# Keys and values staged in DRAM with a row's four tiles one behind the other

## The chip, the cores and the metric

The kernel runs on one core of a Trainium2 chip. The metric is the device time of one execution in microseconds; lower is better. The kernel before was run three times: median 568.12 us, from 563.62 to 568.17 us.

## The reference, cut to what matters

The input x is 32 sequences of 256 tokens of 128 features, float32. Four layers follow one another, each with a layer norm in front and a residual behind: windowed softmax attention (16 query heads, 2 key/value heads of 8 features), a feed-forward layer whose inner matrices are butterflies, linear attention, and the same feed-forward layer again. The change touches the first one alone:

```
q = (x @ Wq + bq) -> 16 heads of 8;  k = (x @ Wk + bk), v = (x @ Wv + bv) -> 2 heads of 8
k, v are padded by 16 zero tokens on both sides of the sequence
block of 32 queries n attends the 64 padded keys 32n .. 32n+63, masked to u in [t, t+32)
out = softmax(q k^T over those) v ;  x = x + out @ Wo + bo
```

Each group of 8 query heads shares one key head, and neighbouring windows overlap by half.

## The kernel before, in words

The 8192 tokens are cut into 16 groups of 512 (four tiles of 128 tokens, two sequences). The program is a software pipeline written out by hand: every engine has a function `turn(t)`, and in turn t it does a step of group t - lag, in an order fixed in the code. Turns 0 to 5 or so fill the pipeline (and TensorE composes the butterfly matrices, products named X, beside it); after them each turn has the same work of about ten groups' stages, and the last turns drain it. Engines wait for each other by counting semaphores (`Count`).

Keys and values of a group take this way. TensorE forms them for the four tiles, one below the other, in one PSUM bank (`attention_kv`, line 616): tile j stands in partitions 32j to 32j+31, of which the first 16 are key features, the other 16 value features, and each row holds 160 tokens (128 and the 16 on either side). VectorE adds the bias and clears the padding into `kv_t` [128, 160] (`attention_kv_out`, line 1020). SyncE stores `kv_t` to a DRAM tensor `kv_rows`, in two alternating copies (`store_keys`, line 326). When the store has landed, SyncE reads it back twice: `spread_keys` (line 335) with eight transfers, one for each query head h of a key head, that put the 16 key rows in partitions h, h+8, ... of `kx`, four tiles side by side, so each row of 640 numbers comes in four pieces of 160 numbers (640 B); and `spread_values` (line 347), one turn later, with eight transfers of 8 rows with four pieces of 64 numbers (256 B). `scores` on TensorE (line 531, products W.S0 to W.S3) reads `kx`; its first one of a group, W.S0, waits for all eight key transfers.

SyncE issues every transfer of the steady pipeline itself, in this order in each turn: the probabilities of tiles 2 and 3 copied between neighbouring partitions (`spread_probs`, line 355, four transfers of 32 partitions with 2 KB each a tile), values, store of keys and values, store of the result (`store_y`, line 362), probabilities of tile 0, keys, probabilities of tile 1, load of x (line 309). Each waits first for its own condition and so holds back all that stand behind it: `spread_probs(g, 0)` for ScalarE's exponentials (line 852), `spread_keys` for the landing of the store and for the last scores product of the group before (W.S3), the load of x for GpSimd (line 429). GpSimd masks the copied probabilities (`probs_parted`, line 459), which TensorE then multiplies with the values (line 548). VectorE works on the scores in line 1070 and after.

In turn 2 `spread_keys` also sends two loads of constants (`load_constants`); the first transfer of values waits for one of them. The first column of the table of rows below tells the time from the start of the profiled span.

Of the kernel before, what the change touches and what calls it, by code (L numbers as in the profile page):

```python
# [8 lines left out]
F32 = mybir.dt.float32  # L9
# [6 lines left out]
HEADS, KV, HD = 16, 2, 8  # L16
HPK = HEADS // KV
# [3 lines left out]
P = 128  # L21
TSPAN = P + 2 * PAD
TILES = 4
# [93 lines left out]
def due(t, lag, first=0, last=NG - 1):  # L117

    return (t - lag,) if first <= t - lag <= last else ()
# [24 lines left out]
def window_and_linear_attention_with_butterfly_ffn(  # L144
    nc, x, first_c, later_c, outer_c, vones_c, w_exp_t, w_con, up_m, down_m, out,
):
    with ExitStack() as ctx:
        def sb(name, shape, dt=F32):
            return ctx.enter_context(nc.sbuf_tensor(name, shape, dt))

        def sem(name):
            return ctx.enter_context(nc.semaphore(name))
# [49 lines left out]
        kv_t = sb("kv_t", [P, TSPAN])  # L202
        kx = sb("kx", [P, HPK, TILES * TSPAN])
# [58 lines left out]
        pool_step = Count(sem("pool_step"), POOL_STEPS)  # L262
        normed = Count(sem("normed"), NORMED)
        biased = Count(sem("biased"), BIASED)
        kv_rows = nc.dram_tensor("kv_rows", [2, P, TSPAN], F32).ap()
        kv_out = Count(sem("kv_out"), [("P.ko", 0)], 16)
        x_in = [sem(f"x_in{i}") for i in range(2)]
        kx_in = Count(sem("kx_in"), [("P.kx", 0)], 16 * HPK)
        spread = [Count(sem(f"spread{j}"), [(f"W.d{j}", 0)], 16 * 4) for j in range(TILES)]
# [6 lines left out]
        def x_of(g, s):  # L276
            return x_p[g % 2] if s == "P" else xs[s]
# [3 lines left out]

        def keys_of(g):

            return kv_rows[g % 2].rearrange("(j r) n -> r j n", j=TILES)[0:KV * HD]

        def values_of(g, kv):
            return kv_rows[g % 2].rearrange("(j r) n -> r j n", j=TILES)[KV * HD + kv * HD:KV * HD + (kv + 1) * HD]

        def outer_stage(eng, src, dst, tmp, coef, stage, step, seen):

# [11 lines left out]
        @block.sync  # L302
        def _(sp):
            def load_x(g):

                sp.wait_ge(normed.sem, normed.after(g - 2, "P.xn"))
                sp.wait_ge(biased.sem, biased.after(g - 2, "P.xb"))
                if g != 1:
                    sp.dma_start(x_of(g, "P")[:], x_v[g]).then_inc(x_in[g % 2], 16)
                if g == 0:  # L310
                    sp.dma_start(first[:], first_c).then_inc(first_in, 16)
                    sp.dma_start(x_of(1, "P")[:], x_v[1]).then_inc(x_in[1], 16)

            def load_constants():

                sp.dma_start(vx_t[:], vones_c.rearrange("p (a n) -> p a n", a=1).to_broadcast([P, TILES, P])
                             ).then_inc(vones_in, 16)
                sp.dma_start(later[:], later_c).then_inc(later_in, 16)

            def store_keys(g):  # L320

                own = drained[BANK["P.kv"]]
                sp.wait_ge(own.sem, own.after(g, "P.kv"))
                sp.wait_ge(kx_in.sem, kx_in.after(g - 2, "P.kx"))
                sp.wait_ge(v_in.sem, v_in.after(g - 2, "P.v"))
                sp.dma_start(kv_rows[g % 2], kv_t[:]).then_inc(kv_out.sem, 16)

            def spread_keys(g):

                sp.wait_ge(kv_out.sem, kv_out.after(g, "P.ko"))  # L330
                sp.wait_ge(kx_cleared, 2)

                sp.wait_ge(product.sem, product.after(g - 1, *SCORES))
                for h in range(HPK):
                    sp.dma_start(kx[h:P:HPK, h].rearrange("d (j n) -> d j n", j=TILES), keys_of(g)
                                 ).then_inc(kx_in.sem, 16)
                if g == 0:
                    load_constants()

            def spread_values(g):  # L340
                sp.wait_ge(kv_out.sem, kv_out.after(g, "P.ko"))
                sp.wait_ge(vones_in, 16)
                sp.wait_ge(vec.sem, vec.after(g - 1, "W.vx"))
                for i in range(4):
                    for kv in range(KV):
                        c = WINDOW[kv][i & ~1] + i % PARTS
                        sp.dma_start(vx_t[32 * i:32 * i + HD, :, kv * SPAN:(kv + 1) * SPAN],
                                     values_of(g, kv)[:, :, 32 * c:32 * c + SPAN]).then_inc(v_in.sem, 16)

            def spread_probs(g, j):  # L350

                sp.wait_ge(probs.sem, probs.after(g, f"W.E{j}"))
                for i in range(4):
                    own, other = slice(32 * i, 32 * i + 32), slice(32 * (i ^ 1), 32 * (i ^ 1) + 32)
                    sp.dma_start(probs_t[other, j, i % PAIR].rearrange("p k h t -> p (k h t)"),
                                 probs_t[own, j, i % PAIR].rearrange("p k h t -> p (k h t)")
                                 ).then_inc(spread[j].sem, 16)

            def store_y(g):
                own = drained[BANK["G.down"]]  # L360
                sp.wait_ge(own.sem, own.after(g, "G.down"))
                sp.dma_start(y_v[g], xs["G"][:]).then_inc(y_out.sem, 16)

            def turn(t):
                for g in due(t, 4):
                    spread_probs(g, 2)
                    spread_probs(g, 3)
                for g in due(t, 3):
                    spread_values(g)
                for g in due(t, 2):  # L370
                    store_keys(g)
                for g in due(t, 8):
                    store_y(g)
                for g in due(t, 3):
                    spread_probs(g, 0)
                for g in due(t, 2):
                    spread_keys(g)
                for g in due(t, 3):
                    spread_probs(g, 1)
                for g in due(t, 0):  # L380
                    load_x(g)

            for t in range(TURNS):
                turn(t)
            sp.wait_ge(y_out.sem, 16 * NG)
# [965 lines left out]
```

## Time and profile before

| | |
|---|---|
| median of 3 runs | 568.12 us (563.62 to 568.17) |
| profiled execution | 568.07 us, of which the span is 566.3 us |
| TensorE (PE) busy | 521.8 us, 92% of the span |
| GpSimd (POOL) | 451.9 us, 80% |
| VectorE (DVE) | 436.6 us, 77% |
| ScalarE (ACT) | 352.2 us, 62% |
| 16 DMA engines | mean 69 GB/s; SyncE's queue took 23.9% of their time |
| granted TensorE clock | 0.988 on average |

Engines are named as the profile does: PE for TensorE's products, PEld for its weight loads, SPq for SyncE's sequencer, which issues the transfers. A row of an issue tells how long the sequencer was at it, not when the data landed. "x8" in a row of the timeline means that eight such instructions stood in it one behind the other. A bracket at its end tells how long the engine had been idle before and what ended that.

### The profile page before, as it was taken

The page shows a single profiled execution, that of the slowest core. Times are in us where ns is not written, and L with a number is a line of the kernel's source. Part 1 is how long each engine was busy: PE and PEld are TensorE (multiplying, and loading weights), DVE is VectorE, ACT ScalarE, POOL GpSimd, SP SyncE. Part 2 cuts the span into 40 slices and gives each one's busy share as a digit, 9 for nine tenths or more (in the row PEclk, how much of TensorE's full clock was granted, in tenths as well). Part 3 has the DMA queues.
Part 4 walks back from the last instruction along what each step waited for, and adds up shares of the span by engine and source line. Part 5 has one row for each costly group of instructions (what it writes and reads, how often), then busy time and mean ns, then how long its engine had stood idle before and what let it go on. Part 6 is the DMA issues. An engine that isn't in the chain of part 4 may idle for free.

```text
span 566.3 us, 14624 instructions
## 1 busy us (share of the span) xinstructions
PE 521.8 (92%) x5048; PEld 344.3 (61%) x5048; DVE 436.6 (77%) x1256; ACT 352.2 (62%) x570; POOL 451.9 (80%) x651
## 2 busy tenths in 40 slices
PE   3866888979999999999999999999999999999876
PEld 2623344546666676766667667566676767677654
DVE  7277979998898989889898888888988888664330
ACT  1323464755876767676776685876767676836632
POOL 6343788989898998999999989898998787877531
PEclk9969999998999999999999999999999999999999
DMA  8414233231222232222223232222222222100001
GB/s 312 139 46 99 62 79 89 59 80 44 68 69 65 58 77 69 68 69 70 71 71 77 68 79 68 63 68 65 57 71 58 69 56 66 39 20 20 2 20 37
DMA packets 50186, 39.14 MB, mean 69 GB/s; under 512 B 12480, under 2 KB 39616, under 8 KB 50112
## 3 DMA queue, kind: packets, MB, share of 16 engines
q1 hardware_dynamic: 47664, 33.99, 23.9%
q10 hardware_dynamic: 2448, 4.22, 2.1%
q8 instruction: 40, 0.66, 0.5%
q14 instruction: 34, 0.28, 0.2%
HBM read 15.89 MB, written 5.51 MB: 38 GB/s over the span
## 4 chain that ended last, share of the span: by engine, by line
PE 79%; DVE 8%; POOL 5%; issue 3%; ACT 2%; ACTq 2%; SPq 1%; DMA 0%; DVEq 0%; POOLq 0%
PE ring L563 20%; PE ring L575 18%; PE ps_s L531 9%; PE ring L512 6%; PE ring L586 5%; PE ps_o L548 4%; PE ring L606 4%; PE ring L646 3%; PE ring L623 2%; POOL probs_t L459 2%; PE ring L595 2%; PE ring L666 1%; DVE merged L1083 1%; PE ring L616 1%; DVE ps_s L1070 1%
## 5 line engine op out<-in xcount | busy, mean ns | idle before, releaser
L459 POOL TENSOR_TENSOR probs_t<-probs_t,first 128x1024 f32<-128x1024 f32 x64 | 151.5, 2368 | 10.8 <-DMA probs_t<-probs_t 10.8
L852 ACT ACTIVATE probs_t<-merged_t 128x1024 f32<-128x1024 f32 x64 | 67.1, 1048 | 54.2 <-DVE merged_t L1090 46.2
L833 ACT ACT_TABLE_LOAD x58 | 74.4, 1283 | 10.9 <-issue 9.8
L531 PE MATMUL ps_s<-kx,q_t 64*32 64x512 f32 x1024 | 71.5, 615 | 8.0 <-DVE merged L1083 5.3
L563 PE MATMUL ring<-xT_G,w1b 128*128 128x512 f32 x128 | 66.3, 608 | 1.7 <-ACT xT_G L821 1.6
L575 PEld LDWEIGHTS ring<-w,hid_G 128*128 128x128 f32 x512 | 59.5, 192 | 10.0 <-issue 6.7
L575 PE MATMUL ring<-w,hid_G 128*128 128x128 f32 x512 | 60.0, 275 | 1.7 <-ACT hid_G L843 1.7
L563 PE MATMUL ring<-xT_F,w1b 128*128 128x512 f32 x128 | 59.9, 611 | 0.4 <-ACT xT_F L821 0.4
L575 PE MATMUL ring<-w,hid_F 128*128 128x128 f32 x512 | 60.0, 275 | 0.0
L575 PEld LDWEIGHTS ring<-w,hid_F 128*128 128x128 f32 x512 | 58.6, 192 | 0.5 <-issue 0.4
L843 ACT ACTIVATE hid_G<-ring,b 128x512 f32<-128x512 f32 x64 | 43.5, 681 | 17.1 <-PE ring L563 17.1
L1070 DVE COPY_PREDICATED ps_s<-first,ps_s 128x512 f32<-128x512 uint32 x64 | 43.7, 684 | 7.9 <-PE ps_s L531 7.9
L843 ACT ACTIVATE hid_F<-ring,b 128x512 f32<-128x512 f32 x64 | 43.4, 682 | 9.3 <-PE ring L563 7.8
L1097 DVE STREAM_TRANSPOSE ps_o<-ps_o 128x512 f32<-128x512 f32 x64 | 45.7, 714 | 0.2 <-PE ps_o L548 0.2
L548 PE MATMUL ps_o<-probs_t,vx 64*32 64x256 f32 x1024 | 42.3, 387 | 3.7 <-POOL probs_t L459 2.0
L1077 DVE TENSOR_REDUCE rowmax<-ps_s 128x16 f32<-128x512 f32 x64 | 43.1, 673 | 2.4 <-issue 0.2
L1083 DVE TENSOR_TENSOR merged<-ps_s,rowmax 128x512 f32<-128x512 f32 x64 | 43.8, 685 | 1.3
L1090 DVE STREAM_TRANSPOSE merged_t<-merged 128x512 f32<-128x512 f32 x64 | 44.5, 695 | 0.4
L563 PEld LDWEIGHTS ring<-xT_F,w1b 128*128 128x128 f32 x128 | 23.3, 192 | 30.3 <-issue 29.4
L563 PEld LDWEIGHTS ring<-xT_G,w1b 128*128 128x128 f32 x128 | 20.7, 190 | 22.5 <-ACT xT_G L821 12.4
L548 PEld LDWEIGHTS ps_o<-probs_t,vx 64*32 64x32 f32 x1024 | 15.2, 106 | 30.0 <-issue 21.8
L606 PEld LDWEIGHTS ring<-later,xT_L 128*128 128x128 f32 x128 | 22.9, 189 | 15.4 <-issue 11.3
(116 smaller groups left out, 1080.6 us busy)
## 6 DMA issues: line engine op xcount, KB each, us to landing
probs_t<-probs_t SPq DMA_DIRECT2D x256, 64.0 KB, 2.0
kx<-kv_rows SPq DMA_DIRECT2D x128, 40.0 KB, 2.2
x_P<-in_x SPq DMA_DIRECT2D x16, 256.0 KB, 3.3
out_x<-x_G SPq DMA_DIRECT2D x16, 256.0 KB, 2.4
vx_t<-kv_rows SPq DMA_DIRECT2D x128, 8.0 KB
up_s<-in_up_m ACTq DMA_DIRECT2D x7, 256.0 KB, 7.7
down_s<-in_down_m ACTq DMA_DIRECT2D x7, 256.0 KB, 7.7
kv_rows<-kv_t SPq DMA_DIRECT2D x16, 80.0 KB, 1.7
```

The costliest lines, as they stand in the source:

```text
L459: nc.gpsimd.tensor_tensor(parts, parts, keep.rearrange("p (a t) -> p a t", a=1).to_broadcast([P, PAIR * HEADS, WIN]), ALU.mult).then_inc(p ...
L531: last = nc.tensor.matmul(ps_s[32 * i:32 * i + 32, a], q_t[half, P * j + 32 * c:P * j + 32 * c + 32], kx[half, :, TSPAN * j + 32 * c:TSPAN ...
L548: last = nc.tensor.matmul(ps_o[32 * c:32 * c + 32, a, 0:HPK * WIN], vx[rows, j, a, s], probs_t[rows, j, s, a], start=True, stop=True)
L563: nc.tensor.matmul(bank(name)[:], w1b[:, P * c:P * (c + 1)], x_t[s][:], start=True, stop=True).then_inc(product.sem, 1)
L575: last = nc.tensor.matmul(bank(name)[:, P * j:P * (j + 1)], hid[s][:, c, P * j:P * (j + 1)], w2[:, c], start=(c == 0), stop=(c == CH - 1))
L606: last = nc.tensor.matmul(bank(name)[:, 2 * P * i:2 * P * (i + 1)], x_t["L"][:, P * j:P * (j + 1)], wl_s[:, P:3 * P], start=True, stop=True)
L833: nc.scalar.activation(unused[:, i:i + 1], half[0:1, 0:1], function)
L843: nc.scalar.activation(hid[s][:, c], bank(name)[:], ACT.Gelu, bias=b1[:, c:c + 1]).then_inc(drained[BANK[name]].sem, 1)
L852: nc.scalar.activation(probs_t[:, j].rearrange("p s k h t -> p s (k h t)"), scores.to_broadcast([P, PAIR, HEADS * WIN]), ACT.Exp).then_inc ...
L1070: nc.vector.copy_predicated(merged_s, last_half.bitcast(mybir.dt.uint32).rearrange("p (a t) -> p a t", a=1) .to_broadcast([P, HEADS, WIN]) ...
L1083: nc.vector.tensor_tensor(merged[:, j % 2].rearrange("p k h t -> p (k h) t"), halves()[0], m, ALU.subtract).then_inc(drained["S"].sem, 1)
L1097: nc.vector.transpose(ps_o[:, :, 0:HPK * WIN], ps_o[:, :, 0:HPK * WIN]).then_inc(vec.sem, 1)
```

## The change

The DRAM tensor gets 32 rows of 640 numbers in place of 128 rows of 160, so that the four tiles of a feature stand one behind the other in its row. The store becomes four transfers, one a tile (32 partitions of 640 B each, to rows that are 2560 B apart), and the semaphore that tells of it counts 64 instead of 16 a group. A key transfer reads 16 rows of 2560 B whole. A value transfer reads the same pieces as before from other places. SyncE's order and everything on the other engines stay.

```diff
-        kv_rows = nc.dram_tensor("kv_rows", [2, P, TSPAN], F32).ap()
-        kv_out = Count(sem("kv_out"), [("P.ko", 0)], 16)
+        kv_rows = nc.dram_tensor("kv_rows", [2, 2 * KV * HD, TILES * TSPAN], F32).ap()
+        kv_out = Count(sem("kv_out"), [("P.ko", 0)], 16 * TILES)
...
         def keys_of(g):
 
-            return kv_rows[g % 2].rearrange("(j r) n -> r j n", j=TILES)[0:KV * HD]
+            return kv_rows[g % 2][0:KV * HD]
 
         def values_of(g, kv):
-            return kv_rows[g % 2].rearrange("(j r) n -> r j n", j=TILES)[KV * HD + kv * HD:KV * HD + (kv + 1) * HD]
+            return kv_rows[g % 2][KV * HD + kv * HD:KV * HD + (kv + 1) * HD].rearrange("r (j n) -> r j n", j=TILES)
...
                 sp.wait_ge(v_in.sem, v_in.after(g - 2, "P.v"))
-                sp.dma_start(kv_rows[g % 2], kv_t[:]).then_inc(kv_out.sem, 16)
+                for j in range(TILES):
+                    sp.dma_start(kv_rows[g % 2][:, TSPAN * j:TSPAN * (j + 1)], kv_t[32 * j:32 * j + 32]
+                                 ).then_inc(kv_out.sem, 16)
...
                 for h in range(HPK):
-                    sp.dma_start(kx[h:P:HPK, h].rearrange("d (j n) -> d j n", j=TILES), keys_of(g)
+                    sp.dma_start(kx[h:P:HPK, h], keys_of(g)
                                  ).then_inc(kx_in.sem, 16)
```

## Rows read from the trace of the kernel before

**Rows 1.** The page, part 1: busy time, share of the span, instructions.

```profile
PE 521.8 (92%) x5048; PEld 344.3 (61%) x5048; DVE 436.6 (77%) x1256; ACT 352.2 (62%) x570; POOL 451.9 (80%) x651
```

**Rows 2.** Stretches: us, then each engine's busy time, TensorE's clock, DMA share, GB/s.

```profile
20.00:40.00 20.00, 15.21 (x118) 9.76 (x126) 9.10 (x21) 5.95 (x11) 6.35 (x14) 0.83 0.35 94
...
255.00:285.00 30.00, 30.00 (x309) 20.18 (x308) 25.99 (x77) 21.61 (x36) 27.59 (x41) 1.00 0.28 70
```

**Rows 3.** The page, part 6: transfers, KB each, median us from issue to landing.

```profile
probs_t<-probs_t SPq DMA_DIRECT2D x256, 64.0 KB, 2.0
kx<-kv_rows SPq DMA_DIRECT2D x128, 40.0 KB, 2.2
...
kv_rows<-kv_t SPq DMA_DIRECT2D x16, 80.0 KB, 1.7
```

**Rows 4.** Issues by source line: sequencer's time ns min/median/max, first and last start.

```profile
L335 SPq DMA_DIRECT2D kx<-kv_rows x128: 542/595/1899, 18.7 to 451.7; - x128
...
L347 SPq DMA_DIRECT2D vx_t<-kv_rows x128: 264/301/1347, 27.0 to 469.4; - x128
...
L326 SPq DMA_DIRECT2D kv_rows<-kv_t x16: 337/349/1008, 17.1 to 440.2; - x16
...
L355 SPq DMA_DIRECT2D probs_t<-probs_t x256: 507/591/1807, 33.3 to 493.9; - x128
```

**Rows 5.** Timeline from 289 us, a full turn: start, length, engine, line, operation.

```profile
288.21 0.35 SPq L326 DMA_DIRECT2D kv_rows<-kv_t  x1
...
288.60 0.43 SPq L362 DMA_DIRECT2D out_x<-x_G  x1
...
289.84 2.42 SPq L355 DMA_DIRECT2D probs_t<-probs_t  x4
...
295.25 5.06 SPq L335 DMA_DIRECT2D kx<-kv_rows  x8
...
300.10 2.36 POOL L459 TENSOR_TENSOR probs_t<-probs_t,first 128x1024 f32<-128x1024 f32 x1
...
303.47 1.06 PE L531 MATMUL ps_s<-kx,q_t 64*32 64x512 f32 x16
```

**Rows 6.** Timeline of the fill, group 0's store to its masked probabilities.

```profile
17.10 0.34 SPq L326 DMA_DIRECT2D kv_rows<-kv_t  x1
...
18.74 5.11 SPq L335 DMA_DIRECT2D kx<-kv_rows  x8
...
27.01 2.73 SPq L347 DMA_DIRECT2D vx_t<-kv_rows  x8
...
27.76 1.09 PE L531 MATMUL ps_s<-kx,q_t 64*32 64x512 f32 x16
...
33.30 2.49 SPq L355 DMA_DIRECT2D probs_t<-probs_t  x4
...
34.97 1.96 PE L531 MATMUL ps_s<-kx,q_t 64*32 64x512 f32 x16 [2.52 <-DVE merged L1083]
...
40.43 2.36 POOL L459 TENSOR_TENSOR probs_t<-probs_t,first 128x1024 f32<-128x1024 f32 x1
```

**Rows 7.** Timeline of the fill, scores that wait for keys of groups 1, 2, 4.

```profile
48.28 1.09 PE L531 MATMUL ps_s<-kx,q_t 64*32 64x512 f32 x16 [2.25 <-DMA kx<-kv_rows]
...
58.35 0.35 SPq L326 DMA_DIRECT2D kv_rows<-kv_t  x1
...
60.32 2.41 SPq L355 DMA_DIRECT2D probs_t<-probs_t  x4
...
62.85 5.52 SPq L335 DMA_DIRECT2D kx<-kv_rows  x8
...
70.86 1.09 PE L531 MATMUL ps_s<-kx,q_t 64*32 64x512 f32 x16 [0.45 <-DMA kx<-kv_rows]
...
72.79 0.69 DVE L1070 COPY_PREDICATED ps_s<-first,ps_s 128x512 f32<-128x512 uint32 x1
...
121.86 0.18 PEld L531 LDWEIGHTS ps_s<-kx,q_t 64*32 64x32 f32 x16 [0.30 <-DMA kx<-kv_rows]
```

## The prediction

> **What bounds the kernel now.** I read the busy times first [rows 1]: TensorE has 522 of 566 us and no other engine comes near. Then the stretches [rows 2]: from 255 to 285 us TensorE is busy for all 30.00 us, with GpSimd at 27.6 and VectorE at 26.0; from 20 to 40 us it has only 15.2 of 20. So the time is a steady part in which TensorE alone counts, and a fill of some 130 us in which single waits count. A change on SyncE's queue moves the time in two ways only: in the fill, where TensorE, VectorE or GpSimd waits for a transfer, and in the steady turns, if a transfer comes so late that TensorE stops. The timeline tells which transfers those can be. In the fill, scores wait for keys three times [rows 7]: 2.25 us at 48.28, 0.45 at 70.86, 0.30 (of the weight load) at 121.86. In a steady turn nothing waits for them: the keys' last issue ends at 300.31, 2.2 us from issue to landing [rows 3] puts it at 301.9, and the scores that use them start at 303.47 [rows 5], when TensorE comes to them.
>
> **The store, as seen by SyncE.** One issue of 0.35 us [rows 4] goes, four come, each of 32 partitions. No such store is in the trace. The nearest rows from both sides: the present 128-partition store, 0.35, and the copy of probabilities, which also has 32 partitions, 0.59 [rows 4]. Eight key issues take 5.06 us and four copies 2.42 [rows 5], so with the gaps between them an issue of the longer kind costs 0.64. Lower bound: 3 x 0.39 = 1.2 us more; upper: 4 x 0.64 - 0.39 = 2.2 us more. I take 2.2, since the copy agrees in what decides between them, as far as rows show it: issue time follows neither bytes (80 KB in 0.35, 40 KB in 0.60) nor pieces (128 in 0.35, 32 of the copy in 0.59), but transfers of 16 and 32 partitions take twice those of 8 (0.30), and only those of all 128 are cheap.
>
> **The store, until it has landed.** Before: 1.63 us at 17.10 (the keys start at 18.74 the moment it has landed) and 1.7 in the median [rows 3, 6]. After: the fourth is issued 1.9 us after the first and lands 1.6 to 2.0 us later (the store's and the copy's time, rows 3): 3.5 to 3.9, so 1.9 to 2.3 us later than now; with the cheap issue 1.2.
>
> **What is queued behind it.** In a steady turn it is the store of the result, the copies of tile 0, the keys, the copies of tile 1 and the load of x. SyncE is idle from 289.03 to 289.84 and from 292.26 to 295.25 [rows 5], 3.8 us in all, and the later store takes 2.2 of it: the copies of tile 0 start 1.4 us late, and the keys not at all, since they wait for the last scores of the group before. The store will have landed at 288.21 + 3.9 = 292.1, 3 us before the keys want it. The copies have 2.0 us to land, until 294.3 before and 295.7 after; GpSimd takes them at 300.10. The copies of tile 1 are behind the keys and don't move. The stored result and the values have a turn of slack. Steady turns: 0. What covers it is SyncE's 3.8 us of idle time; without that each late microsecond of keys would meet 1.5 us of slack at the scores (301.9 to 303.47) before TensorE stops.
>
> **The fill, group 0** [rows 6]. The keys follow the landing directly: 18.74 becomes up to 21.0. Their last landing was about 23.85 - 0.6 + 2.3 = 25.6, and the scores start at 27.76, so 2.2 us of slack against 1.9 to 2.3: 0 to 0.1 us late. Behind the keys the constants go 2.2 us later, and so do the values that wait for them (27.01) and the next store; that ends at about 34.6, where the copies of tile 0 stood at 33.30. 1.3 us later they still land at 34.6 + 2.5 + 1.4 = 38.5, before GpSimd takes them at 40.43. Cost: 0.1 us.
>
> **The fill, group 2** [rows 7]. SyncE's idle time between store and keys is only 60.32 - 58.70 = 1.6 and 62.85 - 62.73 = 0.1, so the keys come 0.5 us late, and the scores start at 71.4 and end at 72.4. VectorE takes them at 72.79, because it is not free before. Cost: 0, hidden by VectorE's work before line 1070; were that gone, 0.5. In the other turns the two gaps hold 2.2 us or more.
>
> **The key transfers.** 128 issues before and after, of 40 KB each, with 16 pieces for 64. Issue time: by the paragraph on the store unchanged (0.60). Landing: 2.2 us with four pieces for each of 16 rows, 2.0 for the copy, which moves more bytes in fewer pieces [rows 3]. So the gain lies between 0 and 0.2 us; I take 0.1, and it counts where scores wait for keys, three times: -0.3 us. The value transfers keep their pieces: 0.
>
> **Sum.** 568.07 (profiled execution, span 566.3 and 1.8 around it) + 0.1 - 0.3 = **567.9 us**. The median of the runs is 568.12, so the profiled execution is a typical one; one of the three runs took 563.62 without any change to the kernel.
>
> The rows show stores and copies in flight together: four copies issued 0.6 us apart [rows 4, 5] with 2.0 us to landing each [rows 3]. The Trainium skill ("DMA: Bandwidth & Descriptors", Rules for kernel authors) speaks against this change: two transfers to disjoint halves of the partitions serialize, so one of 128 partitions should be used instead. By that rule the four stores would be a loss as the second rival below has it, while by the rows it is hidden.
>
> **Rival 1, the key issues get cheaper with their pieces.** For it: 64 pieces in 0.60, 32 pieces of a value transfer in 0.30 [rows 4]. Against it: the copy's 32 pieces take 0.59, and the store's 128 take 0.35. Then at least 8 x 0.3 = 2.4 us of each round of keys goes, and at 48.28 the whole wait of 2.25 us, at 70.86 0.45 [rows 7]; what is late next is TensorE's own order. Time: 568.07 - 2.25 - 0.45 - 0.3 = 565.1. Chance 0.10.
>
> **Rival 2, slower: the four stores land one behind another,** 2.0 us each as a 32-partition copy needs, so at 8.0 instead of 1.6 us. It decides in the fill, from 2.2 us of delay on. Group 0's scores come 6.4 - 2.2 = 4.2 us late. Group 2's store lands at 66.4 where the keys stood at 62.85: 3.5 us, less the 0.8 us between the end of the scores at 71.95 and VectorE's start at 72.79, so 2.7. In a steady turn 288.21 + 8.0 = 296.2 is 1.0 us behind 295.25, inside the 1.5 of slack. 568.07 + 6.9 = 575.0. Chance 0.04.
>
> **Rival 3, the fill falls into step with the clock in another way.** At 34.97 the same 16 products take 1.96 us that take 1.09 at 27.76 [rows 6], and the granted clock from 20 to 40 us is 0.83 [rows 2]: it was at 1.2 instead of 2.4 GHz, behind a stretch in which TensorE waited for VectorE (2.52 us idle in that row). Two such scores products in a row lie on the chain that ends last, 0.9 us each, and what follows adds as much again. That a run at 563.6 stands beside two at 568.1 fits such a thing, though no row proves it. The shifts of up to 2 us in the fill can turn it either way: 563.6 (chance 0.14), or 3 to 4 us slower, 571.5 (chance 0.04).
>
> **Rival 4, the transfers are cut into the old pieces anyway**: then the -0.3 is gone, 568.2, within the forecast's own range.
>
> **Numbers.** A measurement of this kernel tells 1% (5.7 us) from no change. Forecast 567.9 with 0.66, its own range 567.0 to 569.0 (store issues between the bounds, key landing between 0 and 0.2, runs within 0.3); rivals as above; 0.02 for something unseen. Range 563.3 to 570.0: it takes in rival 1 and the fast side of rival 3, and leaves out rival 2 and the slow side. Faster by over 1%: 0.03 (rivals 1 and 3 together). Slower by over 1%: 0.04 (rival 2). Within 1%: 0.93.
>
> **What would show it.** Four rows at line 326's place of 0.59 each, 0.35 if I am wrong about 32 partitions. Store to keys in group 0: 3.5 to 3.9 us. Key issues still 5.06 for eight, landing 2.1. Steady keys still waiting for W.S3, with SyncE's two gaps together at 1.6 instead of 3.8 us. TensorE still 30.00 of 30 us. Key issues at 0.3 us would speak for rival 1, keys in group 0 after 23 us for rival 2. The forecast fails if a store of 32 partitions to spread rows takes far longer than any row here, or if the scores of group 0 at 27.76 open a new low stretch of the clock.

## The result, and the profile after

The changed kernel takes 570.38 us (median of 8 runs, 568.47 to 572.48) where the kernel before took 567.07 beside it (563.62 to 568.76): a ratio of 1.0045, 95% interval 1.0024 to 1.0067. (The ratios in this text are those on record and not the quotient of the two medians, which here is 1.0058.) Slower, by half of one per cent. The forecast was 567.9 with a range that ended at 570.0, so the direction of the move was missed and the time lies just outside. The profiled execution took 570.3 us with a span of 568.5.

The issues by source line answer to [rows 4] (SyncE's time for one, min/median/max in ns). In the changed kernel:

```profile
L327 SPq DMA_DIRECT2D kv_rows<-kv_t x64: 318/421/775, 16.4 to 446.7; - x64
...
L337 SPq DMA_DIRECT2D kx<-kv_rows x128: 492/589/1587, 19.3 to 454.5; - x128
...
L349 SPq DMA_DIRECT2D vx_t<-kv_rows x128: 637/649/1383, 27.2 to 474.1; - x128
```

The store costs four issues of 0.42 us, between the two bounds of the prediction, and the keys 0.59, as forecast. The third row is what the prediction had at nothing: a value transfer now takes 0.649 us of SyncE where it took 0.301, though it moves the same 32 pieces of 256 B to the same place. Eight of them a turn make 2.8 us, twice what the stores add.

The timeline of a steady turn shows what that does to the queue; it answers to [rows 5]:

```profile
287.73 5.59 SPq L349 DMA_DIRECT2D vx_t<-kv_rows  x8
...
293.43 1.77 SPq L327 DMA_DIRECT2D kv_rows<-kv_t  x4
295.24 0.42 SPq L364 DMA_DIRECT2D out_x<-x_G  x1
...
295.71 3.48 SPq L357 DMA_DIRECT2D probs_t<-probs_t  x4
...
296.27 1.06 PE L533 MATMUL ps_s<-kx,q_t 64*32 64x512 f32 x16
299.30 4.95 SPq L337 DMA_DIRECT2D kx<-kv_rows  x8
...
305.80 0.18 PEld L533 LDWEIGHTS ps_s<-kx,q_t 64*32 64x32 f32 x16 [0.35 <-DMA kx<-kv_rows]
305.80 1.09 PE L533 MATMUL ps_s<-kx,q_t 64*32 64x512 f32 x16
```

SyncE had 3.8 us of idle time between the store and the keys; now each row begins within 0.12 us of the last one's end. The last scores of the group before, for which the keys used to wait, end at 297.33, and the keys start at 299.30, 2.0 us later: they now wait for their turn on the queue. This is the latest of the ten turns; in the others the keys start 0.7 to 1.6 us behind those scores, where it was 0.2 before in all but one. The scores that read them start at 305.80 as the keys land (their last issue began at 303.66, and the median to landing is 2.2 us), where they had 1.5 us to spare.

Where the time went: between the first scores of group 5 and those of group 15 lie ten steady turns. Before:

```profile
152.25 1.06 PE L531 MATMUL ps_s<-kx,q_t 64*32 64x512 f32 x16
...
454.79 1.09 PE L531 MATMUL ps_s<-kx,q_t 64*32 64x512 f32 x16
```

After:

```profile
153.85 1.09 PE L533 MATMUL ps_s<-kx,q_t 64*32 64x512 f32 x16
...
457.11 1.09 PE L533 MATMUL ps_s<-kx,q_t 64*32 64x512 f32 x16
```

302.54 us became 303.26: the steady part lost 0.7 us, the fill before it 1.6, and the drain behind is the same (566.3 - 454.8 = 111.5, 568.5 - 457.1 = 111.4). These are two single executions; the table at the end of the experiments has the same two stretches for all. In the fill the keys of groups 3 and 4 now come directly behind the copies (91.89 to 92.00, 118.40 to 118.52), and TensorE stops for them:

```profile
74.06 1.06 PE L533 MATMUL ps_s<-kx,q_t 64*32 64x512 f32 x16
...
89.42 2.47 SPq L357 DMA_DIRECT2D probs_t<-probs_t  x4
92.00 4.94 SPq L337 DMA_DIRECT2D kx<-kv_rows  x8
...
98.54 1.09 PE L533 MATMUL ps_s<-kx,q_t 64*32 64x512 f32 x16 [0.35 <-DMA kx<-kv_rows]
...
115.93 2.47 SPq L357 DMA_DIRECT2D probs_t<-probs_t  x4
...
118.52 5.95 SPq L337 DMA_DIRECT2D kx<-kv_rows  x8
...
126.05 1.09 PE L533 MATMUL ps_s<-kx,q_t 64*32 64x512 f32 x16 [1.40 <-DMA kx<-kv_rows]
```

The first row is from group 2: its scores stood at 70.86 before and are 3.2 us late already, without a wait for keys. The part on the fill below comes back to it.

The table of waits (us in total, times, longest) has for these products, first before (weight loads), then after (weight loads and products):

```profile
PEld ps_s L531 <- DMA kx<-kv_rows: 4.0, 3, 2.7
...
PEld ps_s L533 <- DMA kx<-kv_rows: 8.3, 8, 3.6
...
PE ps_s L533 <- DMA kx<-kv_rows: 4.9, 3, 3.1
```

Group 0 cost nothing, as forecast, though the delay was smaller than the 3.5 to 3.9 us of the prediction: the store is issued at 16.44, the keys at 19.30, 2.9 us instead of 1.6, and its scores don't wait for them.

```profile
16.44 1.73 SPq L327 DMA_DIRECT2D kv_rows<-kv_t  x4
19.30 4.99 SPq L337 DMA_DIRECT2D kx<-kv_rows  x8
...
27.09 1.09 PE L533 MATMUL ps_s<-kx,q_t 64*32 64x512 f32 x16
```

### The profile page after: what moved, and what is told of

Its sections match the earlier page's. It is cut to its first block, busy times and chain, and to the rows that moved or that the text cites. A ratio compares the mean times of both kernels' runs of the same rounds, so it can differ in the third digit from the quotient of the medians.

```text
span 568.5 us, 14672 instructions
## 1 busy us (share of the span) xinstructions
PE 524.6 (92%) x5048; PEld 345.4 (61%) x5048; DVE 436.9 (77%) x1256; ACT 352.2 (62%) x570; POOL 450.9 (79%) x651
## 4 chain that ended last, share of the span: by engine, by line
PE 71%; SPq 7%; POOL 6%; DVE 5%; issue 3%; ACT 3%; DMA 2%; ACTq 1%; DVEq 0%; POOLq 0%
PE ring L577 16%; PE ring L565 16%; PE ps_s L533 9%; PE ring L514 6%; PE ring L608 5%; PE ring L588 4%; PE ps_o L550 4%; SPq L337 3%; PE ring L648 2%; SPq L357 2%; PE ring L597 2%; POOL probs_t L461 2%; PE ring L625 2%; SPq L349 2%; DMA kx<-kv_rows 2%
## 5 line engine op out<-in xcount | busy, mean ns | idle before, releaser
L533 PE MATMUL ps_s<-kx,q_t 64*32 64x512 f32 x1024 | 73.1, 629 | 10.4 <-DVE merged L1085 5.5
L565 PEld LDWEIGHTS ring<-xT_G,w1b 128*128 128x128 f32 x128 | 20.7, 190 | 22.4 <-ACT xT_G L823 12.4
```

Source lines behind the costliest of these rows:

```text
L533: last = nc.tensor.matmul(ps_s[32 * i:32 * i + 32, a], q_t[half, P * j + 32 * c:P * j + 32 * c + 32], kx[half, :, TSPAN * j + 32 * c:TSPAN ...
L565: nc.tensor.matmul(bank(name)[:], w1b[:, P * c:P * (c + 1)], x_t[s][:], start=True, stop=True).then_inc(product.sem, 1)
```

## The experiments

**Theories.** A: the loss comes through SyncE's queue, and most of it through the dearer value issues. B: it comes from the store in four parts. C: it comes from the larger key pieces. Medians, ratios and intervals are against the kernel before on the same chip.

In the built program the value transfers look different. Their DRAM side, as steps and counts, was `[160, 8], [5120, 4], [1, 64]`: 8 rows, 4 tiles, 64 numbers. In the new layout a row of 640 numbers is exactly four tiles of 160, so rows and tiles are one run of equal steps, and the build writes it as `[160, 32], [1, 1], [1, 64]`, while the SBUF side keeps `8, 4, 64`. This is read from the built programs; a trace doesn't show it.

**e1: the changed kernel with a row pitch of 672 numbers.** Now 8 rows and 4 tiles can't be merged.

```diff
-kv_rows = nc.dram_tensor("kv_rows", [2, 2 * KV * HD, TILES * TSPAN], F32).ap()
+kv_rows = nc.dram_tensor("kv_rows", [2, 2 * KV * HD, TILES * TSPAN + 32], F32).ap()
...
-            return kv_rows[g % 2][0:KV * HD]
+            return kv_rows[g % 2][0:KV * HD, 0:TILES * TSPAN]
...
```

(`values_of` gets the same `0:TILES * TSPAN`.)

> The changed kernel, but a row of the staging tensor is 672 numbers long instead of 640 (32 unused at its end). Its one effect on the transfers: the four tiles of a row no longer follow on the next row's, so the source of a value transfer stays 8 rows of 4 pieces, where it may be taken as 32 equal steps in the changed kernel. Theory A (the loss comes from the value transfers, whose issue went from 0.301 to 0.649 us, eight a turn, so 2.8 us of SyncE's time a turn): issue back at about 0.30, SyncE has idle time before the keys again, and the time is within 0.1% of before, 567.1 to 567.9 us where before is 567.1. Theory B (the loss comes from the store in four parts, 1.4 us more of SyncE's time and a landing 1.2 us later): still 0.4 to 0.5% slower than before, about 569.5 to 570.4. Theory C (the key transfers of 2560 B pieces do it): the same as B.

568.5 us against 568.17; ratio 1.0000 (0.9975 to 1.0026). Its value issues, and a turn of its queue:

```profile
L349 SPq DMA_DIRECT2D vx_t<-kv_rows x128: 288/301/693, 27.9 to 469.9; - x128
```

```profile
288.76 1.71 SPq L327 DMA_DIRECT2D kv_rows<-kv_t  x4
290.51 0.42 SPq L364 DMA_DIRECT2D out_x<-x_G  x1
290.98 2.43 SPq L357 DMA_DIRECT2D probs_t<-probs_t  x4
...
295.79 4.92 SPq L337 DMA_DIRECT2D kx<-kv_rows  x8
```

Idle time is back: 2.4 us before the keys. The kernel keeps the four stores and the whole-row keys, so neither B nor C makes a loss by itself that can be told. One number in the shape of a DRAM tensor takes the loss away.

**e2: the kernel before with its store in four.**

```diff
-                sp.dma_start(kv_rows[g % 2], kv_t[:]).then_inc(kv_out.sem, 16)
+                for j in range(TILES):
+                    rows = slice(32 * j, 32 * j + 32)
+                    sp.dma_start(kv_rows[g % 2][rows], kv_t[rows]).then_inc(kv_out.sem, 16)
```

> The kernel before with its store alone in four parts (32 partitions each, old layout; keys and values read as before). Theory A (value issues): within 0.15% of before. Theory B (the store in four): 0.4 to 0.5% slower, as the changed kernel. Theory C (key pieces): the same as before. SyncE's issues for the store: 4 x 0.42 us as in the changed kernel, if their cost is not a matter of the spread rows in DRAM; 0.35 or less each, if it is.

568.01 us, ratio 1.0000 (0.9981 to 1.002), issues of 0.418 us. Theory B alone is out, and the spread rows in DRAM are not what makes a store of 32 partitions cost 0.42.

**e3: the kernel before with eight more value-like transfers a turn.**

```diff
+                for n in range(8):
+                    i, kv = n // KV, n % KV
+                    sp.dma_start(spare[32 * i:32 * i + HD, :, kv * SPAN:(kv + 1) * SPAN],
+                                 values_of(g, kv)[:, :, 0:SPAN]).then_inc(spare_in.sem, 16)
```

> The kernel before with eight more transfers a turn behind the value transfers, of the same shape (8 partitions, 4 pieces of 256 B), from the same DRAM rows into an unused tile: 8 x 0.34 = 2.8 us more of SyncE's time at the place where the changed kernel's value transfers take 2.8 us more, with neither the four stores nor the other layout. Theory A: slower by most of the loss, 0.2 to 0.4% (1 to 2.5 us), and keys that follow directly on the copies of tile 0 in many turns. Theories B and C: the same as before, within 0.1%.

567.92 us, ratio 1.0006 (0.9989 to 1.0024). Theory A as I had put it, with most of the loss in the value issues alone, missed: 2.8 us more on the queue cost nothing that can be measured, and the keys follow directly on the copies in few turns. What it left open is whether the 1.4 of the stores and the 2.8 of the values cost only together, as the 3.8 us of idle time would have it. That is what e6 to e11 ask.

**e4: issues by shape.** Behind the last result come groups of four transfers each.

> The kernel before, and behind the last result 16 groups of four transfers each that move nothing that is used, for the sequencer's time of an issue by shape. If the source that can be taken as one run of equal steps costs the time (theory A's cause): 8 partitions of 4 pieces at a row pitch of 672 numbers 0.30 us, at 640 numbers 0.65; the same pair with 16 partitions apart in the same direction. If the number of engines sets it: 8 partitions 0.30 in both, 16 and 32 partitions 0.59, 128 partitions 0.35. Stores of 32 partitions 0.42 whether their rows in DRAM are 640 B or 2 KB long, if the direction SBUF to DRAM decides.

SyncE's time of one, min/median/max in ns. In order: 8 partitions of 4 pieces at pitch 672 and at 640; the same with 16 partitions; 16 whole rows of 640 numbers; 32, 64 and 128 partitions of 160 numbers; an SBUF to SBUF copy of 32 partitions; a store of 128 partitions.

```profile
L409 SPq DMA_DIRECT2D kx<-in_x x4: 296/304/308, 568.8 to 569.8; - x4
...
L412 SPq DMA_DIRECT2D kx<-in_x x4: 672/692/789, 571.3 to 573.6; - x4
...
L418 SPq DMA_DIRECT2D kx<-in_x x4: 333/419/426, 578.6 to 579.9; - x4
...
L421 SPq DMA_DIRECT2D kx<-in_x x4: 593/596/609, 581.7 to 583.6; - x4
...
L424 SPq DMA_DIRECT2D kx<-in_x x4: 327/420/421, 585.6 to 586.9; - x4
...
L430 SPq DMA_DIRECT2D kx<-in_x x4: 310/421/423, 592.1 to 593.4; - x4
...
L433 SPq DMA_DIRECT2D kx<-in_x x4: 522/596/598, 595.3 to 597.2; - x4
...
L436 SPq DMA_DIRECT2D kx<-in_x x4: 362/432/434, 599.4 to 600.7; - x4
...
L439 SPq DMA_DIRECT2D kx<-kx x4: 557/590/592, 602.8 to 604.6; - x4
...
L451 SPq DMA_DIRECT2D probe_d<-kx x4: 338/432/433, 616.7 to 618.0; - x4
```

The pair at the top isolates what makes the value issue dear: the same bytes and pieces cost 0.30 us at one pitch and 0.69 at the other. With 16 partitions the pair is 0.42 and 0.60. There are two classes, 0.30 to 0.43 and 0.59 to 0.69. In the built program every transfer of the dear class lacks a mark that all of the cheap class carry, and whose name speaks of descriptors prepared ahead: the merged sources, the 64 partitions, the SBUF to SBUF copies, and the key transfers, whose SBUF side steps 8 partitions at a time. Mark and class go together in every shape here, but no run changes the mark alone, so it is a clue and not a shown cause. Stores of 32 partitions took 0.42 with rows of 640 B and of 2 KB, as the loads of 32 did, so the direction doesn't set the 0.42. The rule in my prediction, cheap at 8 and at 128 partitions and dear between, is wrong: 16 whole rows into adjacent partitions take 0.42.

**e5: the changed kernel again, in the same job as e6 to e8.**

> The changed kernel once more, beside the next three. Every theory: 0.3 to 0.6% slower than before.

571.35 us against 569.3; ratio 1.0048 (1.0023 to 1.0074).

**e6: e2 and e3 together, in the old layout** (both diffs above).

> The kernel before (old layout, old key and value transfers) with both burdens at once: its store in four parts and the eight more transfers of 8 partitions into an unused tile, 1.4 + 2.8 = 4.2 us more of SyncE's time a turn. If what counts is that the sum passes the 3.8 us that SyncE has idle between the store and the keys, while neither part alone does: 0.3 to 0.6% slower, like the changed kernel, with keys directly behind the copies of tile 0 in every turn. If the changed kernel's loss has to do with its value transfers in another way than their length, or with its layout: the same as before, within 0.15%.

573.16 us against 569.3, ratio 1.0091 (1.0055 to 1.0127). A turn:

```profile
291.74 2.71 SPq L357 DMA_DIRECT2D spare<-kv_rows  x8
294.61 1.71 SPq L331 DMA_DIRECT2D kv_rows<-kv_t  x4
296.37 0.42 SPq L372 DMA_DIRECT2D out_x<-x_G  x1
296.84 3.90 SPq L365 DMA_DIRECT2D probs_t<-probs_t  x4
...
300.84 5.07 SPq L340 DMA_DIRECT2D kx<-kv_rows  x8
...
307.55 1.09 PE L542 MATMUL ps_s<-kx,q_t 64*32 64x512 f32 x16 [0.27 <-DMA kx<-kv_rows]
```

Neither part cost anything alone; together they cost, with keys directly behind the copies and scores that wait for them, as in the changed kernel and without its layout. The loss is a matter of the sum. It is larger than the changed kernel's, and the intervals of e5 and e6 overlap only between 1.0055 and 1.0074.

**e7 and e11: sixteen and twelve more transfers** in e3's diff, for 5.6 and 4.2 us.

> The kernel before with sixteen more transfers of 8 partitions a turn, 5.6 us more of SyncE's time. By the idle time of 3.8 us: the keys come 1.8 us late in steady turns, against about 1.5 us of slack at the scores that wait for them, so slower than the changed kernel, 0.6 to 1.2%. If time on SyncE's queue doesn't set the loss: no slower than the changed kernel.

596.22 us against 569.3, ratio 1.0457 (1.0423 to 1.049).

> The kernel before with twelve more transfers of 8 partitions a turn, 4.2 us of SyncE's time, the same dose as the changed kernel's and as e6's, but in the cheap form alone. By the idle time of 3.8 us: 0.3 to 1.0% slower, between eight more (nothing) and sixteen more (4.6%). If the store in parts was needed for the loss: the same as before.

576.14 us against 567.83, ratio 1.0165 (1.0123 to 1.0207). Both miss their figures on the high side: my idle time gave the place of the bend and not the slope behind it. The expectation for e7 set the 1.5 us of slack at the scores against the lateness of every turn; if lateness is carried from turn to turn, that slack can pay only once. The ten steady turns of e7 took 320.35 us for 302.54, 1.8 us more each, and 5.6 - 3.8 is 1.8. That is an account after the fact, and no run tests it. In e7, from 150 to 450 us TensorE is busy for 289.6 us where it was for 299.4:

```profile
150.00:450.00 300.00, 289.63 (x2887) 191.47 (x2886) 247.26 (x723) 206.11 (x329) 262.40 (x379) 0.99 0.28 69
```

**e8 and e10: the new layout at pitch 672 with one store.** Its DRAM side goes tile by tile.

```diff
+                sp.dma_start(kv_rows[g % 2][:, 0:TILES * TSPAN].rearrange("r (j n) -> j r n", j=TILES), kv_t[:]
+                             ).then_inc(kv_out.sem, 16)
```

> New layout at a row pitch of 672 numbers, keys in 16 whole rows, and the store in one transfer again, whose DRAM side goes tile by tile. SyncE's issue about 0.6 us instead of 4 x 0.42, so 0.25 us more than before. By theory A the time of before, within 0.15%, or 0.1 to 0.3 us less if the larger key pieces land 0.1 us sooner. If its landing (four slices of the DRAM side) takes over 2 us longer than the 1.6 of before, group 0's keys are late and 1 to 2 us are lost.

566.9 us against 569.3, ratio 0.9972 (0.9948 to 0.9996). It looked like a gain, so it was run again:

> The kernel of e8 once more (new layout at pitch 672, one store, cheap value transfers), since its ratio of 0.9972 was near the edge of what can be told. If it is a gain: 0.996 to 0.999; if it was chance: within 0.1% of 1.

567.62 us against 567.83, ratio 1.0000 (0.9974 to 1.0025). The two together don't show a gain. The keys in 16 pieces are worth nothing that can be told here.

**e9: the changed kernel with one store**, so the dear value transfers stand alone (e8's diff at pitch 640).

> The changed kernel with its store in one transfer again (DRAM side tile by tile, 0.59 us to issue), at the row pitch of 640 numbers, so the value transfers still cost 0.65 us each. SyncE's time a turn over before: 2.8 for the values and 0.25 for the store, 3.0 us, less than its 3.8 us of idle time. If only the sum counts: within 0.2% of before. If the value transfers alone make the loss: 0.3 to 0.5% slower.

567.64 us against 567.83, ratio 1.0016 (0.9988 to 1.0043). The interval reaches nearly to the changed kernel's 1.0045, so the time alone doesn't rule a loss out; the queue says more. The value issues have 0.655 us as a median, and SyncE still idles 0.6 us before the keys in the turn shown:

```profile
284.48 5.65 SPq L348 DMA_DIRECT2D vx_t<-kv_rows  x8
...
290.24 0.55 SPq L326 DMA_DIRECT2D kv_rows<-kv_t  x1
290.83 0.47 SPq L363 DMA_DIRECT2D out_x<-x_G  x1
291.35 2.47 SPq L356 DMA_DIRECT2D probs_t<-probs_t  x4
...
294.45 4.91 SPq L336 DMA_DIRECT2D kx<-kv_rows  x8
```

By the time added to SyncE's turn, the runs line up so. The last two columns are from the one profiled execution of each: when the first scores of group 5 start, and how long the ten steady turns from there to those of group 15 take.

| kernel | added us a turn | ratio to before | group 5 at us | ten turns, us |
|---|---|---|---|---|
| before | 0 | 1 | 152.3 | 302.54 |
| e8, e10: one store, pitch 672 | 0.25 | 0.9972, 1.0000 | 153.7, 151.6 | 302.51, 302.54 |
| e1: pitch 672, e2: four stores | 1.4 | 1.0000, 1.0000 | 152.8, 151.8 | 302.55, 302.56 |
| e3: eight more | 2.8 | 1.0006 | 152.3 | 302.75 |
| e9: dear values, one store | 3.0 | 1.0016 | 151.4 | 302.53 |
| the changed kernel, e5 | 1.4 + 2.8 = 4.2 | 1.0045, 1.0048 | 153.9, 156.4 | 303.26, 303.19 |
| e6: four stores and eight more | 4.2 | 1.0091 | 154.2 | 305.57 |
| e11: twelve more | 4.2 | 1.0165 | 156.2 | 304.85 |
| e7: sixteen more | 5.6 | 1.0457 | 165.4 | 320.35 |

The ten turns show the bend by themselves: up to 3.0 us added they stay within 0.21 us of before, and behind that every kernel is longer, the changed one by 0.7 in both its profiles. The fill is not so steady: below the bend it ends anywhere between 151.4 and 153.7, so the 1.6 us of one pair is no measure of the loss there.

## Why the prediction was wrong

**The step that failed** is the last sentence of the part on the key transfers: "The value transfers keep their pieces: 0." The pieces did stay. What changed is the cost of the issue, which I took as a matter of the destination's partitions. SyncE's added time was forecast as 2.2 us a turn and was 4.2: 1.4 for the stores (4 x 0.44 against 0.39; I had taken the upper bound, the trace is near the lower) and 2.8 for values. Undoing the 2.8 alone (e1) brings the time of before, and so does undoing most of the 1.4 alone (e9), within an interval that is wide.

**The mechanism behind that was in the prediction and is right:** what covers an addition to this queue is SyncE's 3.8 us of idle time between store and keys. Below it no loss can be told (0.25 to 3.0 us), above it TensorE begins to wait. Had the value issue been known, 4.2 against 3.8 would have turned the forecast to slower, though not told by how much.

**The steady part** was forecast at 0 and lost 0.7 us of the 2.2 between the two profiled executions. The reserve of 1.5 us at the scores takes most of the lateness: keys 1.8 us later than before (2.0 instead of 0.2 us behind the last scores) made a 0.35 us stop of the weight loads in the turn shown.

**The fill** was forecast at +0.1 for its delays and lost 1.6 us in that pair. Group 0 had its 0 as forecast. For group 2 the text has the keys 0.5 us late and hidden; they were not late, starting at 65.55 with SyncE idle for 0.65 us before them and 0.1 us after the last scores of group 1 had ended. Keys came late in groups 3 and 4, where the two idle gaps "hold 2.2 us or more", which is true (2.6 and 4.1), and not 4.2: TensorE waited 0.35 us at 98.54 and 1.40 at 126.05, where it had waited 0 and, by its weight load, 0.30. But these waits are not the whole of it. Group 2's scores, which waited for no keys, already started 3.2 us late, groups 3 and 4 3.0 and 4.2 us late, and group 5 only 1.6. The granted clock goes with the first and the last step: from 40 to 60 us it was 0.91 before and 0.74 in the changed kernel, from 60 to 80 us 1.00 and 0.91, and from 120 to 140 us 0.91 before and 1.00 in the changed kernel.

**The landing of the store** was forecast 1.9 to 2.3 us later and came 1.2 later (2.9 after 1.6 us in group 0), since the cheap issue held. (The sum for group 0 also takes 2.3 us for the landing of keys, where the row has 2.2; nothing hangs on it.) **The landing of keys**: 2.2 us in the median of the changed kernel, 2.1 in e1. The 0.1 us a wait that I had counted as -0.3 is not to be seen in any ratio.

**The rivals.** Rival 1 (key issues cheaper by their pieces) is out: 0.589 for 0.595. Rival 2 (stores landing one behind another) is out: the keys started 2.9 us after the first store, not 8.0. So what the prediction cites from the Trainium skill ("DMA: Bandwidth & Descriptors", Rules for kernel authors), that two transfers to disjoint halves of the partitions serialize and one of 128 partitions should be used, doesn't show at this size: four stores of 20 KB, issued 0.44 us apart, landed 1.5 us after their issue in the median, and e2, with its four parts, took the time of before. Rival 3 (the clock in the fill) is seen in the traces, and does not explain why e1, e5 and e6 come out as they do over 6 to 12 runs each. From 40 to 60 us some of the changed kernel's products ran at 1.2 GHz, behind stops of 2.5 and 3.1 us. The first row is the kernel before, the rest is the changed one:

```profile
40.00:60.00 20.00, 14.35 (x158) 6.58 (x143) 14.68 (x34) 7.42 (x12) 10.91 (x8) 0.91 0.31 77
...
20.00:40.00 20.00, 15.25 (x125) 9.20 (x123) 9.71 (x21) 6.51 (x12) 6.51 (x15) 0.83 0.35 94
40.00:60.00 20.00, 14.84 (x146) 7.77 (x138) 11.87 (x28) 5.92 (x10) 10.31 (x6) 0.74 0.28 72
...
34.31 1.96 PE L533 MATMUL ps_s<-kx,q_t 64*32 64x512 f32 x16 [2.51 <-DVE merged L1085]
...
47.11 1.94 PE L533 MATMUL ps_s<-kx,q_t 64*32 64x512 f32 x13 [3.11 <-DMA kx<-kv_rows]
```

The runs of the kernel before alone spread over 563.7 to 569.9 us in one job, so ratios of many runs are needed to see half a per cent; what makes that spread, no run shows. How much of the 1.6 us in the fill is waiting for keys and how much is the clock's different place, these runs don't separate.

**Left open.** Three kernels that were given the same 4.2 us of queue time lost 0.45%, 0.91% and 1.65%. A part of it is that the doses were not the same. SyncE's rows between the keys of group 5 and those of group 15, with the gaps of up to 0.2 us between them counted in, make 20.3 us a turn before, 24.4 and 24.5 in the two profiles of the changed kernel, 24.9 in e6 and 25.0 in e11: 4.1 to 4.2 us more in the one and 4.7 in the others, since each of the eleven and twelve more issues has a gap behind it too, and the changed kernel has three more. Why e11 lost more than e6 stays open: their intervals just touch, they ran on different chips, and in the ten steady turns e6 lost more, 3.0 against 2.3 us. Single groups of copies that took 1.0 to 1.5 us longer to issue than the rest (3.90 in e6 and 3.48 in the changed kernel for four, against 2.42) are in the kernel before as well (3.19 at 270.13), and no experiment took them apart.

## What to carry to other kernels

Cost an edit of a layout on every transfer that touches it, those with unchanged pieces too, and look at the steps and counts that the build makes of both sides: a row pitch that is exactly the number of tiles times their step (640 = 4 x 160) lets two dimensions merge on one side alone, and that doubled the issue here; a padded pitch avoided it. Count a queue's idle time in front of the transfer that others wait for, and hold the sum of all additions against it: two additions that are free each on their own can cost together. Count the gap behind each issue with it. Where an unknown price doesn't matter below a threshold, the forecast should say how far off the threshold the sum stands.

## What the runs showed of the hardware that was not expected

- SyncE's time for an issue does not follow bytes, pieces or partitions alone: 0.30 us against 0.69 for 8 partitions of 4 pieces of 256 B, at DRAM pitches of 2688 and 2560 B; 0.42 for 16 and 32 partitions, 0.60 for 64, 0.43 for 128 (medians of four in e4).
- Whole rows of 2560 B in place of four pieces of 640 B changed neither the issue (0.595 to 0.589 us) nor, by more than 0.1 us, the landing (2.2 us).
- Past its idle time the queue's price rises steeply: 1.4 us more in each of 16 turns, from e11 to e7, raised the loss against the kernel before on the same chip from 8.3 to 26.9 us, 18.6 of the 22.4 us that SyncE was given.
